# Expert rows and a bias half loaded before the stage boundary, last scatters without a wait, a late key/value tile ahead of the last rank

## The reference, cut to what matters

```python
x = x + xattn0(layernorm(x), ctx)                 # 8 heads, stage 1 of the kernel
# stage 2: experts, of layer 0
logits = layernorm(x) @ W_gate + b_gate           # 8 experts
_, top_idx = top_k(logits, 2)
y = relu(einsum('bsd,edh->bseh', x_n, W_e) + b_e) # the two chosen experts, mean of both
x = x + y
x = x + xattn1(layernorm(x), ctx)                 # stage 3, needs keys and values of ctx
x = x + ffn1(layernorm(x))                        # stage 4
```

## Time and profile before

| | |
|---|---|
| median of 3 runs | 884.24 us (882.51 to 885.11) |
| the profiled execution's own time | 884.15 us |
| its span, first to last instruction | 882.4 us |
| mean granted TensorE clock | 0.989 of full speed |
| PE busy | 845.8 us, 96% of the span |
| DVE, ACT, POOL busy | 433.5, 346.2 and 284.0 us |

### The profile page before, as it was taken

One profiled execution on the slowest core, in us unless ns is written; L12 is line 12 of the kernel. 1 busy time (PEld: TensorE's weight loads), 2 busy tenths in 40 slices (PEclk: granted clock), 3 DMA queues, 4 the chain that ended last, 5 costly groups with the idle time before them and its releaser, 6 DMA issues.

```text
span 882.4 us, 19749 instructions
## 1 busy us (share of the span) xinstructions
PE 845.8 (96%) x7585; PEld 689.5 (78%) x7585; DVE 433.5 (49%) x839; ACT 346.2 (39%) x567; POOL 284.0 (32%) x401
## 2 busy tenths in 40 slices
PE   5999997899999989999999999999999999999996
PEld 4888877788888867777777788878887888878885
DVE  4999974244444688888888722133221312222112
ACT  3666653233333466666666622222221122211110
POOL 3578884000000778877753321130020002002000
PEclk9999998799999999999999999999999999999999
DMA  8477678595553634554422431010120003010001
GB/s 277 144 252 252 232 251 274 198 333 187 164 163 113 209 111 136 164 147 134 125 58 58 139 118 60 24 33 1 46 87 12 1 13 108 0 63 34 1 0 49
DMA packets 55389, 105.29 MB, mean 119 GB/s; under 512 B 8226, under 2 KB 12322, under 8 KB 55042
## 3 DMA queue, kind: packets, MB, share of 16 engines
q1 hardware_dynamic: 48530, 85.02, 30.2%
q0 software_dynamic: 5120, 16.78, 5.9%
q10 hardware_dynamic: 1648, 2.23, 0.7%
HBM read 68.02 MB, written 35.98 MB: 118 GB/s over the span
## 4 chain that ended last, share of the span: by engine, by line
PE 74%; issue 2%; POOL 2%; ACT 2%; DVE 1%; DMA 0%; SPq 0%; DVEq 0%; ACTq 0%; POOLq 0%
PE c_ps L1277 9%; PE c_ps L1279 9%; PE c_ps L1278 9%; PE c_bank L1801 4%; PE c_bank L1315 3%; PE c_bank L1316 3%; PE c_bank L1321 3%; PE c_bank L1807 3%; PE c_bank L1802 3%; PE c_bank L1865 3%; PE c_ps L1840 2%; PE c_bank L1014 2%; PE c_bank L1015 2%; PE c_bank L1020 2%; PE c_po L1015 2%
## 5 line engine op out<-in xcount | busy, mean ns | idle before, releaser
L1354 DVE SCALAR_TENSOR_TENSOR d_hid<-c_ps,d_b_up,d_silu 128x512 f32<-128x512 f32 (+1 forms) x44 | 33.0, 751 | 227.4 <-PE c_ps L1279 227.4
L1277 PE MATMUL c_ps<-d_nT_hi,gate_up_hi 128*128 128x512 f32 (+1 forms) x352 | 139.9, 398 | 0.0
L1279 PE MATMUL c_ps<-d_nT_hi,gate_up_lo 128*128 128x512 f32 (+1 forms) x352 | 138.6, 394 | 0.0
L1278 PE MATMUL c_ps<-d_nT_lo,gate_up_hi 128*128 128x512 f32 (+1 forms) x352 | 138.3, 393 | 0.0
L1233 ACT ACTIVATE d_silu<-c_ps,d_b_gate 128x512 f32<-128x512 f32 (+1 forms) x44 | 30.3, 689 | 141.6 <-PE c_ps L1279 141.6
L1193 POOL TENSOR_TENSOR late_x<-late_x,d_b_down 128x512 f32<-128x512 f32 x16 | 21.5, 1377 | 187.9 <-DMA late_x<-x_after_attention 187.9
L1279 PEld LDWEIGHTS c_ps<-d_nT_hi,gate_up_lo 128*128 128x128 f32 (+1 forms) x352 | 65.2, 185 | 16.6
L1278 PEld LDWEIGHTS c_ps<-d_nT_lo,gate_up_hi 128*128 128x128 f32 (+1 forms) x352 | 65.4, 186 | 15.8
L1277 PEld LDWEIGHTS c_ps<-d_nT_hi,gate_up_hi 128*128 128x128 f32 (+1 forms) x352 | 65.3, 185 | 15.4
L1240 ACT ACTIVATE d_hid_hi<-d_hid 128x512 fp32r<-128x512 f32 (+1 forms) x44 | 27.8, 632 | 125.7 <-DVE d_hid L1354 125.7
L1044 ACT ACTIVATE b_rowsT_hi<-c_bank 128x512 fp32r<-128x512 f32 x39 | 23.4, 599 | 82.0 <-PE c_bank L1003 82.0
(11 more groups left out here) (308 smaller groups left out, 1930.9 us busy)
## 6 DMA issues: line engine op xcount, KB each, us to landing
b_rows<-expert_rows SPq DMA_DIRECT2D x39, 256.0 KB, 2.9
expert_results<-b_result SPq DMA_DIRECT2D x39, 256.0 KB, 2.5
a_wstage<-L_ffn_W_e SPq DMA_DIRECT2D x16, 512.0 KB, 4.2
late_x<-x_after_attention SPq DMA_DIRECT2D x28, 256.0 KB, 3.7
c_stage<-gate_up SPq DMA_DIRECT2D x16, 344.0 KB
out<-late_x SPq DMA_DIRECT2D x16, 256.0 KB, 2.8
x_after_attention<-late_x SPq DMA_DIRECT2D x12, 256.0 KB, 3.7
c_y_in<-x_after_attention SPq DMA_DIRECT2D x12, 256.0 KB, 2.8
```

Of the source, the lines that this page charges most:

```text
L1277: pe.matmul(bank[0:w, :], gu_hi[:, cols], nT_hi[:, g % 2, k, :], start=k == 0, stop=False)
L1278: pe.matmul(bank[0:w, :], gu_hi[:, cols], nT_lo[:, g % 2, k, :], start=False, stop=False)
L1279: mm = pe.matmul(bank[0:w, :], gu_lo[:, cols], nT_hi[:, g % 2, k, :], start=False, stop=k == KD - 1)
```

## The change

Four edits. (1) The last scatters, those of tiles 12 to 15, don't wait for older scatters. (2) PE's late tile 4 stands before the last rank (tile 15) instead of behind the count. (3) The register loads and the row loads of blocks 0 to 3, and the load of bias half 0, move from SP's queue of stage 2 to the end of its queue of stage 1. The buffers and semaphores for it are made in the outer scope. The register loads wait for step 24 of the table, the row loads for the last low weight part, the last transposed tile and for all scatters. (4) ACT keeps late tile 7 behind the high parts of blocks 0 and 1 instead of ahead of them.

```diff
+ROWS_RING, TABLE_STEPS = 4, 24
-            def load_bias():
+            def load_bias(half):
                 sp.wait_ge(o_made, TILES)
-                sp.wait_ge(w_lo, TILES)
+                if half:
+                    sp.wait_ge(w_lo, TILES)
+                else:
+                    sp.wait_ge(y_made, TILES)
+                    sp.wait_ge(l_made, TILES)
+            def load_first_rows():
+                sp.wait_ge(table_step, TABLE_STEPS)
+                first = [sp.value_load(shared["table"][0:1, 0, b:b + 1], min_val=0, max_val=EXPERTS * REGION - P) for b in range(ROWS_RING)]
+                sp.wait_ge(w_lo, TILES)
+                sp.wait_ge(xt_made, TILES)
+                for i in range(2):
+                    sp.wait_ge(scattered[i], 16 * TILES)
+                for b in range(ROWS_RING):
+                    sp.dma_start(shared["rows"][:, b, :], shared["xs"][bass.ds(first[b], P), :]).then_inc(shared["rows_loaded"][b], 16)
             for i in range(2):
                 sp.wait_ge(x1_stored[i], 8 * TILES)
-                sp.wait_ge(scattered[i], 16 * TILES)
+            load_first_rows()
+            load_bias(0)
             def scatter(t):
-                want(pool, scattered[t % 2], 32 * (t // 2))
+                if t < 2 * KEPT:
+                    want(pool, scattered[t % 2], 32 * (t // 2))
                 if tile(m + 1):
                     make_v(m + 1)
+                if m == TILES + 2:
+                    make_late_k(4)
+                    make_late_v(4)
                 if tile(m - 3) and m >= TILES:
                     make_rank(m - 3)
-            for i in range(4, KV_LATE - 1):
+            for i in range(5, KV_LATE - 1):
         for b in range(BLOCKS + 6):
-            if b < BLOCKS:
+            if RING <= b < BLOCKS:
                 load(b)
-            if b == 1:
-                cols = slice(0, EXPERTS * DIM // 2)
-                sp.dma_start(bias[:, cols], b_e.rearrange("e h -> (e h)")[cols].partition_broadcast(P)).then_inc(shared["bias_loaded"][0], 16)
         for b in range(BLOCKS + 2):
-            if b == 0:
-                keep_last_kv()
             if b < BLOCKS:
                 keep_high(b)
+            if b == 1:
+                keep_last_kv()
```

More of the change, by code:

```diff
@@ L252, in first_attention @@
         shared["bias"] = nc.alloc_sbuf_tensor_at("expert_bias", [P, EXPERTS * DIM], F32, offset=shared["bias_at"])
+        shared["rows"] = nc.alloc_sbuf_tensor_at("expert_rows_in", [P, ROWS_RING, DIM], F32, offset=shared["bias_at"] + 4 * EXPERTS * DIM)
         shared["last_kv"] = wk1, wv1, ctx_in[KV_LATE % 3].rearrange("p (k n) -> p k n", k=KD), kv_stage[(KV_LATE - 1) % 3]
@@ L336, in load_ctxT @@
                 sp.dma_start(ctx_in[(i + 1) % 3], late["ctxT"][KV_EARLY + i, :, :]).then_inc(ctxT_loaded[i % 3], 16)
-            def load_bias():
+            def load_bias(half):
                 sp.wait_ge(o_made, TILES)
-                sp.wait_ge(w_lo, TILES)
-                cols = slice(EXPERTS * DIM // 2, EXPERTS * DIM)
-                rows = shared["b_e"].rearrange("e h -> (e h)")[cols].partition_broadcast(P)
-                sp.dma_start(shared["bias"][:, cols], rows).then_inc(shared["bias_loaded"][1], 16)
+                if half:
[3 more added lines that the diff above has]
+                    sp.wait_ge(l_made, TILES)
+                cols = slice(half * EXPERTS * DIM // 2, (half + 1) * EXPERTS * DIM // 2)
+                rows = shared["b_e"].rearrange("e h -> (e h)")[cols].partition_broadcast(P)
+                sp.dma_start(shared["bias"][:, cols], rows).then_inc(shared["bias_loaded"][half], 16)
+            def load_first_rows():
+                sp.wait_ge(table_step, TABLE_STEPS)
+                first = [sp.value_load(shared["table"][0:1, 0, b:b + 1], min_val=0, max_val=EXPERTS * REGION - P) for b in range(ROWS_RING)]
+                sp.wait_ge(w_lo, TILES)
+                sp.wait_ge(xt_made, TILES)
[3 more added lines that the diff above has]
+                    sp.dma_start(shared["rows"][:, b, :], shared["xs"][bass.ds(first[b], P), :]).then_inc(shared["rows_loaded"][b], 16)
             def store_kv(i):
@@ L374, in _ @@
                 if i == 2:
-                    load_bias()
+                    load_bias(1)
                 store_kv(i)
@@ L925, in _ @@
             then(dve.tensor_copy(shared["table"][:, :, :], table[:, :, :]))
+            assert steps[0] == TABLE_STEPS
             then(dve.tensor_tensor(at_kept2[:, :], at_kept2[:, :], ati[:, :, :].rearrange("p t k -> p (t k)"), ALU.add))
@@ L930, in experts @@
 def experts(nc, c, shared, b_e, late, wq_v, proj_loaded, banks, ident, const_made, kv_bank):
-    RING = 4
+    RING = ROWS_RING
     sem, place = c.sem, Placed(nc, "b_", shared["base"] + 2 * 4 * 2 * EXPERTS * DIM)
@@ L937, in experts @@
     biased, result = sb("biased", [P, 2, DIM]), sb("result", [P, 3, DIM])
[L938 to L941, removed]
+    bias, rows, rows_loaded = shared["bias"], shared["rows"], shared["rows_loaded"]
     pt, py = banks[0:2], banks[2:4]
-    rows_loaded, stored = [sem(f"ex_rows_loaded{i}") for i in range(RING)], [sem(f"ex_stored{i}") for i in range(3)]
+    stored = [sem(f"ex_stored{i}") for i in range(3)]
     t_made, hi_kept, lo_kept, y_made = sem("ex_t_made"), sem("ex_hi_kept"), sem("ex_lo_kept"), sem("ex_y_made")
@@ L2121, in ffn_phase @@
         shared["kv_stored"] = [kept.sem(f"kv_stored{i}") for i in range(3)]
+        shared["rows_loaded"] = [kept.sem(f"rows_loaded{i}") for i in range(ROWS_RING)]
         shared["bias_loaded"] = [kept.sem(f"bias_loaded{i}") for i in range(2)]
```

## The result

| | before | changed |
|---|---|---|
| median of 20 executions | 883.59 us (881.24 to 887.05) | 885.97 us (884.14 to 887.48) |
| the profiled execution's own time | 884.15 us | 886.63 us |
| its span | 882.4 us | 884.9 us |

What follows compares the result with a forecast made beforehand. PE, busy 96% of 882.4 us, was taken as the bound, losing time at the stage boundary to idling and low clock. Stage 2 starting 2.15 us later, then 2.8 us less, gains 0.7: 884.15 becomes 883.4, range 881.0 to 885.7.

Steps and rivals of the forecast that it cites:

- Then tiles 5 and 6 run from about 143.6 to 147.5 ... The store is no longer last; the table is.: End of stage 1: late tiles at full clock, last store started at about 149.0, ahead of the table at 149.75.
- E: Point where PE begins block 2's transposes in stage 2; its shift moves the end; forecast 165.45 instead of 166.14.
- Scatters without waits at nothing: Last scatters on POOL: dropping their waits ends them 3.4 us earlier, worth nothing alone, but lets row loads start early.
- The rank 0.8 later for the late tile: Late tile 4 ahead of the last rank fills the idle 1.57 us; rank 0.8 us later, between 0.4 and 1.2.
- SP's serial work at 6.9 us: From the table to stage 2: register loads, waits, row DMAs, bias, block end sum to 6.9 us; start 2.15 us later.
- 8.8 us from there to E: From stage 2's start to block 2's transposes: 8.8 us, 6.8 of it at low clock, 2.8 us less than before.
- The clock stays up past the rank if the gap is filled: PE at the last rank: without the idle 1.57 us the clock was expected to stay at full speed.
- (b): Rival: the clock falls all the same at the rank, the store is late, stage 2 starts at 159.1; 885.9 us, chance 0.12.
- (a): Rival: early loads pay fully, stage 2 at 156.0, its low clock about half as long; 881.4 us, chance 0.22.
- (c): Rival: SP's serial work is dearer, slow register loads or a late scatter adding 3.4 us; 886.8 us, chance 0.08.

Runs made afterwards that it cites:

- e13: The changed kernel with tile 14's scatter held until tile 15's row numbers are made, without waiting for a landing; 884.50 us, ratio to before 1.0006.
- e6: The kernel before with late tile 4 ahead of the last rank and bias half 1 issued behind the last store; 883.07 us, ratio 0.9970.
- e9: The changed kernel once more, with nothing altered, for a second time and profile; 886.20 us, ratio to before 1.0016.
- e11: The changed kernel with bias half 1 issued behind the row loads instead of ahead of the last stores; 885.06 us, ratio to before 1.0010.
- e1: The kernel before with only late tile 4 moved ahead of the last rank; 884.69 us, ratio 1.0003.
- e5: The changed kernel with the last scatters waiting for older ones again; 884.85 us, ratio to before 0.9993.
- e15: e8 with tile 14's scatter held until tile 15's row numbers are made; 880.25 us in 5 executions, ratio to before 0.9954.
- e4: The kernel before with only the early loads ahead of the boundary and ACT's late tile 7 behind two high parts; 885.52 us, ratio 1.0005.
- e10: The kernel before with only bias half 1 moved behind the last store; 885.30 us, ratio 1.0008.
- e16: e8 once more, unaltered; 882.35 us, ratio to before 0.9975.
- e8: The changed kernel with two rows loaded early, ahead of the last store, bias half 1 behind it, bias half 0 in stage 2; 882.51 us, ratio to before 0.9969.

## Why the prediction was wrong, by its own steps

- **"Then tiles 5 and 6 run from about 143.6 to 147.5 ... The store is no longer last; the table is."** This is the step that failed. The store was put 149.0, 26.9 after the mark, and stands at 30.6 and 30.0. It counted PE and ACT, and took contexts and buffers as ready. Late tiles that move forward need their context loads and stores forward too, and these come behind 1,024 KB of bias and the scatters: in the changed kernel the context load issued at 143.97 let PE start at 151.24, and the store issued at 142.18 let ACT start at 150.03. With the scatter held it is 28.7 (e13), with the old waits and the bias away 27.4 (e6). In the second profile (e9) the context was nearly in time and the late rank brought the clock down instead, with the store at 30.0; in e11 that way alone gave 31.0. With the store 3.7 us behind its place stage 2 starts at 37.7 instead of 34.6, and E stands at 45.9 instead of 43.4 (165.45 less 122.09): 2.5 us late, where the median came out 2.6 above the forecast. So the four-row loads, which the prediction hung on the table at 149.75, started behind a store that was still last. In the first profile the gain from a clock that stays up was spent waiting for transfers.
- **Scatters without waits at nothing.** Wrong by 1.3 us at the start of stage 2: e9 against e13 has the rank 1.1, the table 1.5, that start 1.3 and E 0.8 later. The times, ratios of 1.0016 and 1.0006 with overlapping intervals, don't separate the two. The prediction had named the row, that "PE's results were seen 0.7 to 1.6 us behind its rows", and didn't ask what stood on the other engines then: POOL started the scatters of tile 13 at that moment. With two more of its DMAs there the marks came 2.86 us behind the row instead of 1.65. In the first profile the rank is late by something else: 1.6 us of low clock ahead of the logits row, which no step of mine had.
- **The rank 0.8 later for the late tile.** e1 has it 0.1 later (20.1, 20.0) and e13 too: the tile just about fills the gap.
- **SP's serial work at 6.9 us.** Right: 6.8 from the store's end (154.79) to stage 2's first row (161.56), of it 1.93 for the row DMAs. With the wrong start, though, it gives 37.7 instead of the predicted 34.6 (156.65 less 122.09).
- **8.8 us from there to E.** 8.2 and 7.5 in the two profiles of the changed kernel, 7.3 to 8.3 in all kernels with early rows. Right, 0.6 to 1.3 too dear. PE waits for no row. The clock was low for the start, as said.
- **The clock stays up past the rank if the gap is filled.** The profile after shows 1.00 from 140.0 to 157.0, and the windows of 140 to 150 have 1.00 in e5 and e13, 0.96 in e1, 0.94 in e15; with the gap (before, e4, e10) 0.66 to 0.69. But e16 had an idle 1.77 us ahead of the rank and 1.00 in that window, e6 one of 1.90 ahead of the count and 1.00, and e9, whose rank waited 1.00 us, has 0.83. e1 had a fall after 2.6 us without PE's work and the changed kernel none after 2.81. So filling the gap went with a high clock at the rank, and a single gap of 1.6 to 2.8 us decides nothing by itself: neither my step nor the section of the Trainium skill that the prediction weighed, "Why this matters for your kernels" of "TensorE: Matmul & The Clock Gate", is settled by these runs.
- **The rivals.** (b) gave the measured time, 885.9, with a late store and the 6.9 us behind it, and its marks are near: stage 2 at 37.0 and E at 45.8, where the first profile has 37.7 and 45.9. Its sign, a store that ends more than 0.7 us behind the table, came too, with 2.3 us. That a loss starts at 0.7 isn't shown: in e5 and e13 the store ends about 2 us behind the table, at times like before's. Its cause, the clock falling at the rank, wasn't there in the first profile, and was in e9; that the number fits so well is in part luck. (a) and (c) didn't happen: the register loads took 0.73 us at most.
- **The size.** On the common scale E is 1.8 us later in the first profile of the changed kernel and 0.5 in the second; the timed medians say 2.4 and, by e9's ratio, 1.4. The first profile's remaining 0.7 of 2.5 us is 1.8 ahead of the mark less 1.1 behind E. What makes the executions differ ahead of the mark was not settled: the low stretch of 13.7 to 20.5 lies in code that the change doesn't touch, and I can't say whether the changed kernel falls into it more often.

**A version that beats both.** e15 keeps the late tile, loads the rows of two blocks ahead of the last store, bias half 1 behind it, and holds tile 14's scatter until the rank is through: 880.25 us against 883.94, 0.9954 (0.9936 to 0.9971). These are only 5 executions, 880.02 to 880.98, but all lie below the lowest of e16's eleven, 881.14. The first row of stage 2 is 0.6 us earlier than in before and E 4.3. SP's row loads and last store in it, and PE's first row and point E:

```profile
150.87 0.90 SPq L359 DMA_DIRECT2D expert_rows_in<-expert_rows  x2
151.81 0.43 SPq L363 DMA_DIRECT2D late_keys_values<-a_qT  x1
152.48 0.34 SPq L349 DMA_DIRECT2D expert_bias<-L_ffn_b_e  x1
```

```profile
153.97 2.05 PE L1011 MATMUL c_ps<-a_ctx_own,a_kv_weights 128*128 128x128 f32 x8 [7.10 <-PEq L99]
...
161.99 0.59 PEld L1021 LDWEIGHTS c_bank<-c_ident,expert_rows_in 128*128 128x128 f32 x4
```

e16 against e15, which differ in the held scatter alone: 2.1 us in the medians, 1.8 us of E.

## What to carry to other kernels

Work that is moved ahead of a barrier to warm up the next stage must stand ahead of whatever ends the stage: behind the last store it cost 5 us of start for a way from there to E that was 3.4 to 4.3 us shorter; two rows instead of four, ahead of the store, kept the shorter way and cost 0.9 us of start. Before doing it, try what comes without it: the late tile and the moved bias half alone (e6) gained as much time as the version with the two rows (e8). When compute is moved forward, move its loads and the stores that free its buffers in the same sum, with what is in the queues then. And one profile each is thin ground for marks that a fall of the clock moves by 1.5 us: profile the same kernel twice. A wait that looks idle may be keeping an engine's DMA starts away from a handover on the critical path: before removing it, look at what it will start, and beside what.

## What was not expected of the hardware

While POOL starts indirect DMAs one after another (0.96 us each, 0.30 between), results of PE mostly reach DVE and ACT late: 2.86 and 3.33 us after the end of PE's rows with tile 14's scatter there (e9), 1.47 and 0.57 without it (e13). Eight of nine profiles with this scatter about 18.3 us after the score maximum show it; one, the first of the changed kernel, doesn't (0.03 and 0.04 us). Ends of PE's rows are modelled, so the differences count, 1.4 and 2.8 us. Whether PE's work or only its signal comes late, and by what way POOL has a part in it, the runs don't show; that its transfers do it and not its starts is not excluded either, since holding the scatter moves both. A context load of 256 KB and a store of 200 KB behind the bias half took 7.3 and 7.9 us from issue to the start of the engine that waited, where a row load of 256 KB, with others beside it, took 3.70. With the bias half away (e6) the same context load let PE start 3.9 us behind its issue.
